# Last attention of a four-layer network on one core: 32x32 block transposes on VectorE and block moves by SP's DMAs instead of TensorE transposes

## The reference, cut to what matters

```
def _L3_xattn_ref(x, latents, mask, g_x, b_x, g_l, b_l, Wq, Wkv, Wout, g_o, b_o):
    HEADS = 16; DIM_HEAD = 64
    xn = layer_norm(x, g_x, b_x)
    ln = layer_norm(latents, g_l, b_l)
    q = ln @ Wq
    kv_in = jnp.concatenate([xn, ln], axis=1)
    k, v = jnp.split(kv_in @ Wkv, 2, axis=-1)
    q, k, v = (split_heads(q), split_heads(k), split_heads(v))
    sim = jnp.einsum('bhid,bhjd->bhij', q * DIM_HEAD ** -0.5, k)
    sim = jnp.where(full_mask, sim, max_neg)
    attn = jax.nn.softmax(sim, axis=-1)
    out = jnp.einsum('bhij,bhjd->bhid', attn, v)
    return layer_norm(out @ Wout, g_o, b_o)
```

## Time and profile before

| | |
|---|---|
| median of 3 executions | 2310.82 us (2307.82 to 2314.47) |
| span of the profiled execution | 2306.1 us |
| what lies around the span, taken as the median less the span | 4.7 us |
| PE busy in the span | 2136.2 us (93%) |
| DVE busy | 1394.8 us (60%) |
| ACT busy | 1026.0 us (44%) |
| mean granted clock of TensorE | 0.967 |
| instructions | 34634 |

### The profile page before, as it was taken

The page is one execution under the profiler, slowest core; times in us unless marked ns, Lnnn a source line. Parts: engine busy times, 40 slices in busy tenths (PEclk is TensorE's granted clock), DMA queues, the critical chain, the costliest instruction groups (busy, mean ns, idle before and its releaser), DMA issues.

```text
span 2306.1 us, 34634 instructions
## 1 busy us (share of the span) xinstructions
PE 2136.2 (93%) x13205; PEld 1518.4 (66%) x13205; DVE 1394.8 (60%) x3064; ACT 1026.0 (44%) x2143; POOL 129.1 (6%) x122
## 2 busy tenths in 40 slices
PE   6996998868999799796999999999999999999999
PEld 4874997434999678555566666666666666666654
DVE  5763112672444578687566667666666667676655
ACT  5752442530111522487445444444445444444435
POOL 1002111005122000000100000000000000000000
PEclk8997999889999999898999999999999999999999
DMA  3604897023798600200000000000000000000001
GB/s 116 176 3 170 305 327 242 19 78 136 254 322 273 202 1 1 78 1 1 11 1 1 1 1 1 1 1 1 1 1 1 1 1 1 1 1 1 1 1 37
DMA packets 109264, 159.80 MB, mean 69 GB/s; under 512 B 12555, under 2 KB 85165, under 8 KB 109101
## 3 DMA queue, kind: packets, MB, share of 16 engines
q1 hardware_dynamic: 101805, 134.80, 17.7%
q0 software_dynamic: 7296, 22.78, 3.0%
HBM read 127.64 MB, written 29.91 MB: 68 GB/s over the span
## 4 chain that ended last, share of the span: by engine, by line
PE 51%; DVE 4%; ACT 2%; issue 1%; ACTq 0%; DVEq 0%
PE ps L620 39%; PE ps L1183 10%; PE ps L1190 1%; ACT w_odd L1763 1%; PE ps L1198 1%; DVE small L2488 1%; DVE arena L2510 0%; PE ps L1086 0%; DVE arena L2427 0%; PE ps L1191 0%; DVE w_odd L2426 0%; DVE small L2373 0%; ACT out_feat L1681 0%; PE ps L1095 0%; ACT xn_tok L1624 0%
## 5 line engine op out<-in xcount | busy, mean ns | idle before, releaser
L620 PE MATMUL ps<-arena,w_odd 128*128 128x128 f32 (+4 forms) x2352 | 436.0, 438 | 3.0 <-DVE arena L2165 1.2
L620 PE MATMUL ps<-arena 128*64 128x256 f32 (+4 forms) x3248 | 392.0, 370 | 8.2 <-DVE arena L2296 4.4
L2488 DVE TENSOR_REDUCE small<-ps 128x1 f32<-128x1024 f32 x256 | 312.5, 1221 | 80.7 <-PE ps L620 80.6
L1752 ACT ACTIVATE arena<-ps 128x512 f32<-128x512 f32 x256 | 139.0, 595 | 450.8 <-PE ps L1183 450.7
L620 PEld LDWEIGHTS ps<-arena 128*64 128x64 f32 (+4 forms) x3248 | 258.1, 154 | 120.1 <-issue 22.6
L620 PEld LDWEIGHTS ps<-arena,w_odd 128*128 128x128 f32 (+3 forms) x2352 | 245.1, 187 | 105.0 <-issue 99.7
L1763 ACT ACTIVATE w_odd<-ps,small 128x1101 f32<-128x1101 f32 x256 | 302.5, 1182 | 9.7 <-DVE small L2489 9.0
L1183 PEld LDWEIGHTS ps<-ident,w_odd 128*128 128x128 f32 x2048 | 222.3, 141 | 122.7 <-issue 109.6
L1183 PE MATMUL ps<-ident,w_odd 128*128 128x128 f32 x2048 | 280.6, 277 | 12.0 <-DVE arena L2427 2.9
L2510 DVE COPY arena<-ps 128x512 f32<-128x512 f32 x256 | 164.3, 683 | 5.3 <-PE ps L1183 3.1
L620 PE MATMUL ps<-xn_feat,w_even 128*128 128x512 f32 (+1 forms) x352 | 138.1, 524 | 5.2 <-DVE xn_feat L2409 2.3
(11 more groups left out here) (398 smaller groups left out, 2923.5 us busy)
## 6 DMA issues: line engine op xcount, KB each, us to landing
w_odd<-in_s_w SPq DMA_DIRECT2D x32, 1024.0 KB
w_odd<-in_s_wgu SPq DMA_DIRECT2D x30, 704.0 KB
w_even<-in_s_w SPq DMA_DIRECT2D x15, 1024.0 KB
arena<-expert_rows_in SPq DMA_DIRECT2D x62, 130.0 KB
w_odd<-in_s_wd SPq DMA_DIRECT2D x30, 256.0 KB
out_feat<-in_s_wgu SPq DMA_DIRECT2D x10, 704.0 KB, 4.3
expert_rows_in<-zero_row POOLq DMA_DIRECT2D x1, 5070.0 KB, 34.1
vo_rows<-w_odd SPq DMA_DIRECT2D x8, 616.0 KB
```

The lines of the kernel that those rows point to most:

```text
L620: return pe.matmul(o, lhsT, rhs, start=start, stop=stop, **kw)
L1752: act.activation(s6_pt[g % 2][0][:, 4 * i:4 * i + 4, c0:c0 + P], PS[:, bank, :].rearrange("p (a n) -> p a n", a=4), ACT.Copy).then_inc(r6_ ...
L2488: link(dve.tensor_reduce(m, s6_main[h], AX.X, ALU.max, negate=True))
```

## The change

TensorE no longer transposes the 1024 main columns. In their place

- DVE turns each head's 128x1024 probabilities in 32x32 blocks, in place (`dve.transpose`, two instructions of 1024 columns for each unit). That leaves each block turned within itself, but block (row band i, column band j) still at its old place.
- SP moves the blocks: sixteen DMAs for each unit, one for each pair of 32-partition bands i and j, each with both heads (32 partitions, 2 stretches of 256 values, 64 KB). All sixteen are moved, those with i = j too. They go from `s6_p`/`s6_pm` in w_odd to one of four new tiles `s6_d` in arena. SP first waits (`turned`) for DVE's two transposes of the unit and for the `weigh` that frees the tile; ACT's exponentials of unit u+2 and the group's `weigh` wait (`moved`) for all sixteen to land.
- The key columns come out in another order, and k is made in that order (the `piece` of kind k reads its 256 columns in runs of 32). `weigh` reads the moved blocks with runs of 32 values.
- The copies move: ACT copies the context tiles, the row tiles of stage 7 and all pieces of q, k and v; DVE copies none of them any more. DVE takes the first head's maximum over all 1101 columns in one instruction, without joining.
- `sums_turn` moves from the even iterations to just ahead of `weigh` in the odd ones, and the multiplication after `weigh` to the start of the next even iteration on DVE.

```diff
-        s6_p = [[cut(WO, 1536 + 1104 * (2 * i + h), 1104) for h in range(2)] for i in range(2)]
-        s6_pt = [[cut(AR, 4608 * i + 2304 * h, NKT, 2 * P) for h in range(2)] for i in range(2)]
+        PU = 2240
+        s6_p = [[cut(WO, 1536 + PU * i + (1216 - C) * h, KV) for h in range(2)] for i in range(2)]
+        s6_pm = [cut(WO, 1536 + PU * i, 2, 1216)[:, :, 0:S] for i in range(2)]
+        s6_d = [cut(AR, 2048 * i, 2, S) for i in range(4)]
+        s6_dw = cut(AR, 0, 4, 2, S)
...
+        MOVES = [(i, (i + d) % 4) for d in range(4) for i in range(4)]
+        def moved(eng, u):
+            eng.wait_ge(moved6[u % 4], moved_base + 16 * len(MOVES) * (u // 4 + 1))
+        def turned(eng, u):
+            eng.wait_ge(t6_done, t6_base + 2 * u + 2)
+            if u >= 4:
+                eng.wait_ge(r6_mm, r6_no["v", (u - 4) // 2] + 1)
...
+            for u in range(NU):
+                turned(sp, u)
+                for i, j in MOVES:
+                    sp.dma_start(s6_d[u % 4][32 * j:32 * j + 32, :, 256 * i:256 * i + 256],
+                                 s6_pm[u % 2][32 * i:32 * i + 32, :, 256 * j:256 * j + 256]).then_inc(moved6[u % 4], 16)
...
 def weigh(g):
-                    copied(pe, ("p", 2 * g + 1, 1))
-                    copied(pe, ("p", 2 * g + 1, 3))
+                    moved(pe, 2 * g)
+                    moved(pe, 2 * g + 1)
+                    copied(pe, ("c", 2 * g + 1))
...
                         if u >= 2:
-                            act.wait_ge(r6_mm, r6_no["p", u - 2, 3] + 1)
+                            moved(act, u - 2)
...
+                    if u < NU:
+                        for h in range(2):
+                            dve.wait_ge(a6_p, 2 * u + h + 1)
+                            dve.transpose(s6_pm[u % 2][:, h], s6_pm[u % 2][:, h]).then_inc(t6_done, 1)
```

More of the change, by code:

```diff
@@ L1138, in piece @@
                         for k in range(KD):
-                            last = mm(PS[:, bank, 0:hi - lo], w[:, k, c * P:(c + 1) * P], XNT[:, k, b * S + lo:b * S + hi], start=(k == 0), stop=(k == 1))
+                            rhs = XNT[:, k, b * S:(b + 1) * S]
+                            if kind == "q":
+                                rhs = rhs[:, lo:hi]
+                            else:
+                                rhs = rhs.rearrange("p (i a n) -> p a i n", a=4, i=8)[:, lo // 256:hi // 256]
+                            last = mm(PS[:, bank, 0:hi - lo], w[:, k, c * P:(c + 1) * P], rhs, start=(k == 0), stop=(k == 1))
                         return last
@@ L1174, in scores @@
                     last.then_inc(a6_s, 1)
-                def p_turn(u, i):
-                    pe.wait_ge(a6_p, 2 * u + (1 if i < 2 else 2))
-                    bank = free_bank(("p", u, i))
-                    src = s6_p[u % 2][i // 2]
-                    for j in range(4):
-                        c0 = (i % 2) * 512 + j * P + (C if i >= 2 else 0)
-                        last = pe.transpose(PS[:, bank, j * P:(j + 1) * P], src[:, c0:c0 + P], ident[:, :])
-                    last.then_inc(r6_mm, 1)
                 def ctx_turn(u):
@@ L1210, in weigh @@
                             r = 64 * h
-                            last = mm(PS[r:r + 64, bank, 0:2 * P], s6_v[n % 2][0:rows, i, r:r + 64], s6_pt[g % 2][h][0:rows, i], start=(i == 0), stop=(i == NKT - 1))
+                            if i < NKT - 1:
+                                p = s6_dw[:, s0:s0 + 2, h].rearrange("p u (q i n) -> p u q i n", q=4, i=8)[:, :, :, i]
+                            else:
+                                p = s6_ptc[g % 2][:, h]
+                            last = mm(PS[r:r + 64, bank, 0:2 * P], s6_v[n % 2][0:rows, i, r:r + 64], p, start=(i == 0), stop=(i == NKT - 1))
                     last.then_inc(r6_mm, 1)
@@ L1721, in piece @@
                         return act.activation(s6_q[n % 2][:, lo:hi], PS[:, bank, :], ACT.Copy, scale=DH ** -0.5)
+                    if kind == "k":
+                        return act.activation(s6_k[n % 2][:, lo:hi], PS[:, bank, 0:hi - lo], ACT.Copy)
                     full = min(hi, 8) - lo
@@ L1746, in stage6 @@
                     n, j = u // 8 + 1, u % 8
+                    if u - 1 in N7:
+                        t = N7[u - 1]
+                        bank = filled(("n", t))
+                        act.activation(XNT[:, :, t * P:(t + 1) * P], PS[:, bank, 0:D].rearrange("p (k n) -> p k n", k=KD), ACT.Copy).then_inc(r6_act, 1)
                     if 1 <= u <= NU:
@@ L1749, in stage6 @@
                         g, c0 = v // 2, (v % 2) * P
-                        for i in range(2):
-                            bank = filled(("p", v, i))
-                            act.activation(s6_pt[g % 2][0][:, 4 * i:4 * i + 4, c0:c0 + P], PS[:, bank, :].rearrange("p (a n) -> p a n", a=4), ACT.Copy).then_inc(r6_act, 1)
+                        bank = filled(("c", v))
+                        act.activation(s6_ptc[g % 2][:, :, c0:c0 + P], PS[0:C, bank, 0:2 * P].rearrange("p (h n) -> p h n", h=2), ACT.Copy).then_inc(r6_act, 1)
+                    if not even and 3 <= u < NU + 3:
+                        g = (u - 3) // 2
+                        bank = filled(("r", g))
+                        act.activation(s6_r[g % 2], PS[:, bank, 0:2 * P], ACT.Copy).then_inc(r6_act, 1)
                     if u < NU:
@@ L2472, in stage6 @@
                     even = u % 2 == 0
-                    n, j = u // 8 + 1, u % 8
-                    if even and 2 <= u <= NU:
-                        g = (u - 2) // 2
+                    if even and 4 <= u < NU + 4:
+                        g = (u - 4) // 2
+                        c = (g // 4) % 8
+                        q0 = 2 * P * (g % 4)
+                        bank = filled(("v", g))
+                        copied(dve, ("r", g))
+                        dve.tensor_tensor(s6_ot[c][:, q0:q0 + 2 * P], PS[:, bank, 0:2 * P], s6_r[g % 2], ALU.mult).then_inc(r6_dve, 1)
+                    if not even and 3 <= u < NU + 3:
+                        g = (u - 3) // 2
                         dve.wait_ge(a6_p, 4 * g + 4)
```

76 lines of the change are left out of this document (24 added, 52 removed).

## The result

The changed kernel takes 2584.55 us (median of 4 runs, 2581.60 to 2585.76) against 2310.14 (median of 4, 2307.82 to 2314.47): a ratio of 1.1184, 95% interval 1.1169 to 1.1199. It is 12% slower. The forecast was 2263 us, 2% faster; the time lies above the range, past the rival in which SP is slow (2543).

A forecast was written before the change was run, and what follows sets the result against it. PE, busy 93%, bounded the kernel; after the change SP would. 127 units of 7.89 us plus 25 for projections make 1027 against 1075.3, 48 us less: 2263 us, range 2190 to 2550.

The forecast's parts named there:

- SP is slow: Rival in the last attention: a DMA on few partitions costs SP 0.64 us, kernel 2543 us; chance 0.26.
- the term **SP: Last attention: SP issues 16 DMAs a unit, 0.49 us apart plus 0.05 wait, 7.89 us a unit, and decides.
- The rest of the sum: Stage 6: 127 units of 7.89 us plus 25 make 1027 against 1075.3, 48 us less.
- The loop at 6.6, an odd unit of 6.75: Last attention: the loop through the scores stays at 6.6 us, an odd unit on PE takes 6.75.
- Transposes 1.21: DVE's two added 128x1024 block transposes a unit take 1.21 us each, leaving DVE at 6.1 us a unit.
- Transfers and landing: SP's moves: 3.1 us of transfers a unit hide under 7.89 of issuing; 64 KB lands 1.9 us after issue.
- Projections 25 us: Output projections on PE: six of eight lie before the last mask addition, 4 us each, 25 in all.
- PE's clock: Rival: PE idles in even units and its clock falls; at 0.70 the kernel takes 2363 us; chance 0.05.

## Why the prediction was wrong

The failed step is the term **SP**. Its structure held: SP issues 16 DMAs a unit in order, nothing hides them, and the unit is 16 x s + 0.05. Its value s = 0.49 did not: the moves measured 0.639. The value was taken from the weight loads, whose source lies in DRAM; moves with a source there in one stretch a row came near it (0.464, 0.470, 0.512). With a source in SBUF no move got under 0.633. I compared the form of the destination (stretches, partitions) and never asked about the source, neither its place nor its form: that is the mistake. Over 127 x 16 issues the 0.149 us are 303 us. With them, without the 25 of the projections, which hide at this length of a unit, and with 33 for the long issues and 9 behind the last mask addition, the forecast of 2263 becomes 2583; measured 2584.55.

The rows before held a warning. Against the slow SP the prediction said that the loads of 128 partitions next to those of 64 are as fast as ever. That reading was wrong (the same loads, ns, shortest, median and longest):

```profile
L437 SPq DMA_DIRECT2D w_odd<-in_s_b x3: 586/597/600, 1098.9 to 1101.8; - x3
L437 SPq DMA_DIRECT2D w_odd<-in_s_g x3: 467/471/588, 1100.2 to 1101.3; - x3
```

The last of the three `in_s_b`, at 1101.8 us, covers 128 partitions and took 0.59 us, and so did the first `in_s_g`, on 128 partitions too. The last `in_s_g` covers 64 and took 0.47. So the dear issue was in the kernel before on 128 partitions as well as on 64, and the chance of 0.26 for a price of 0.64 rested on a comparison that does not hold.

- *Rival "SP is slow".* Its price, 0.64, was right, and its 2543 misses by the 33 us of long issues and the 9 us behind the last mask addition: 2585. Its reason, few partitions, was wrong: 32, 64 and 128 partitions cost 0.639, 0.650 and 0.664.
- *The rest of the sum* lacked a term, SP's long issues. With the source in DRAM the kernel stood 48.6 us (at 0.464) and 44.4 us (at 0.470) under the kernel before; the forecast was 48. This is luck: at 0.464 the sum gives 127 x 7.47 + 25 = 974 us, 101 less than before, and the long issues took back 40 of that. A spacing under 0.49 and the missing term cancel (100.36 us for 200 issues are a mean of 0.50).
- *The loop at 6.6, an odd unit of 6.75.* With eight moves a unit took 6.74 us in the middle of the stage (from the 17th to the 49th) and 7.21 over all, projections included.
- *Transposes 1.21.* 1.241 [L2522]; VectorE never became the bound.
- *Transfers and landing.* Hidden, as forecast: a quarter of the bytes gave 7 us, 3 of them in the 127 units. The landing of 1.9 us shows as 2.04 in the chain.
- *Projections 25 us.* Hidden at 10.54 a unit, as the rival had it. They come back as soon as the unit is near 8: with the source in DRAM at 0.464 SP waited 34 us at the ends of units, 24 of them behind the six projections. The prediction's other figure for them is off: it shares 56 us of the kernel before among eight, and only six lie in that stretch.
- *PE's clock* fell to 0.84 in the window. It followed the slower units: at 7.2 us a unit it is 0.99, and at 10.5 PE has room, 349 of 482 us.

## What to carry to other kernels

When work moves from an engine to DMAs, first multiply the number of DMAs of one unit by the spacing of issues on their queue, and take that spacing from issues whose *source* is of the same place and form as the new ones; 0.15 us was worth 300 us here, against 7 us for three quarters of the bytes and 48 us for four times the partitions. Where one queue is the bound, give part of it to others before giving the idea up: ten issues on SP and six copies by an idle engine turned 12% slower into 6% faster.

## What the runs showed of the hardware

- In the last attention a move from SBUF, or from two separate stretches in DRAM, started 0.63 to 0.66 us after the one before; from one stretch in DRAM 0.46 to 0.51. Why, stays open. It is not the long row of issues: with eight moves, where SP waits 1.8 us between units in the median, the first move after the wait took 0.586 us.
- The table doesn't cover other issues of the kernel before. The two weight loads 0.51 apart in the earlier trace rows read two separate stretches a partition, 128 matrix rows apart, and the tiny loads at 0.64 there read one. From SBUF, with one stretch of 4 or 8 KB a partition and a destination in DRAM, issues were cheap: the four of the output took 0.37 to 0.40 us, and a pair of `vo_rows` 0.32 and 0.48, not 0.60. So neither the place nor the form of the source sets the price by itself, and a value for another kernel has to come from issues like its own.

```profile
L613 SPq DMA_DIRECT2D out_dram<-x_res x4: 372/384/395, 2292.8 to 2302.8; - x4
19.48 0.84 SPq L476 DMA_DIRECT2D vo_rows<-w_odd  x2
```

- SP's long distances of 1.0 to 2.0 us come every 27 to 64 issues (42 in 1353 us), and also with the source in DRAM; their cause wasn't looked for.
- A GpSimd copy of 32 partitions x 512 float32 takes 0.61 us, from 32 partitions to the same or to others (3.95 us for six, 5.29 for eight). Beside such copies VectorE's broadcast of 128x256 took 0.67 us and not 0.29; its transposes took no longer.
